# A four-block image model on one core: channels sorted by depth in the convolution attention, bands in two stages, and a linear attention in plain fp32

## The chip, the cores and the metric

One core of a Trainium2 chip. The metric is device time in microseconds (us) of one launch, median of several runs. A profile of one execution lists every instruction with its start and length. Engines: PE is TensorE (PEld its weight loads, which run beside its matmuls), DVE is VectorE, ACT is ScalarE, POOL is GpSimd, SP is SyncE, which only issues DMAs here. SBUF is the on-chip memory with 128 rows, PSUM the accumulator memory with eight banks of 512 fp32 values per row.

## The reference

x has the shape (32, 64, 16, 16): 32 pictures, 64 channels, 256 positions. All is fp32.

```
x = x + pe                                    # pe = pos @ W.T + b, the same for all pictures
x = x + conv_attention(group_norm(x))
t = tokens(x)                                 # (32, 256, 64)
t = t + causal_attend(layer_norm(t))          # softmax scan over the 32 pictures
t = t + mixture(layer_norm(t))                # 16 experts, top 2, hidden 128
t = t + linear_attention(layer_norm(t))
t = t + mixture(layer_norm(t))
```

The two that the change touches most:

```
# conv_attention: 8 heads of depth 8, C = 64
q, k, v = xt @ Wq.T + bq, xt @ Wkv.T + bkv (two halves)
q, k = (relu(q) + 1e-6) / scale, (relu(k) + 1e-6) / scale
q, k = q**3 / |q**3| * |q|, k**3 / |k**3| * |k|
out = per head: (q @ (k.T @ v)) / (q @ sum(k) + 1e-6)
out = out + conv5x5(v, per depth: the same kernel for all heads) + dwc_b
y = out @ Wproj.T + bproj

# linear_attention: 8 heads of 64, N = 256 tokens of a picture
h = x @ qkv_w + qkv_b, seen as q, v of (B, H, 64, N)
attn = sum over n of q[d, n] * lunchbox[d, r] * scale      # (B, H, R, D)
res = einsum('bhrd,bhdn->bhnd', attn, v)                   # a gain per (b, h, d), times v
out = res.reshape(B, N, H * 64) @ proj_w + proj_b
```

## The kernel before, in words

The program is a chain of stages, each a block in which every engine has its own hand-written program; a barrier ends each block. Semaphores order the engines inside a block, and each engine works its list strictly in order. The activations X lie in SBUF with tokens on rows: X[p, q, par, (b c)], where q is a pair of pictures, par the parity of the position, b the picture in the pair and c the channel.

**stage_norm** (L54 to L224) loads x, adds the position term and computes the group norm. DVE sums statistics (L173, L176), the softplus of the scale (L163 to L192), the group means, then the scaled weights into `wqkv` and `wproj` (L203 to L208), the biases into `brow` (L211 to L215), the transposed taps into `rowk` (L217), and the scale of the norm (L219, L220). Then ACT (L142) and DVE (L224) write half each of the normalised `xn`. PE turns the weights (L151, L152), expands the taps (L154) and averages the statistics over pairs of channels (L157).

**stage_qkv** (L227 to L408). PE multiplies `xn` with the weights in plain fp32 (L272) and adds the biases as an fp32r product of two parts (L273), 32 times. DVE takes q and k out (L390), ACT takes v out into V (L334). Squares and sixth powers on ACT (L305, L311), the cube on POOL or, for the last group, on DVE (L364), norms on DVE (L400, L402), roots on ACT (L316, L317), and the factor on DVE and POOL (L371), in four groups. The 5x5 convolution is a matmul of V with band matrices T: PE makes the bands in eight sets of four matmuls (L284) from `rowk` and the selection `sely`, ACT copies them into T (L322), all after the last of the 32 products. After that PE does 16 convolutions (L295), each for one depth d and one output parity: two accumulating fp32 matmuls of 256 columns. The channel of V is (head, depth), so the columns of one depth lie 8 values apart. Two PSUM banks alternate, and convolution k waits until ACT has taken out convolution k - 2 (L328):

```
pe.matmul(ps[:, 4 + k % 2, 0:B * NH], T[:, pj, 2 * d + pi, :],
          V[:, :, pj, d:2 * C:HD], start=(pj == 0), stop=(pj == 1))
```

**stage_attend** (L411 to L564). SP loads a mask and the projection bias, then the expert weights of the first mixture and the zeros of the block buffers. PE makes k.T @ v per pair of pictures (L453), DVE masks it to blocks of heads, BD (L540, L541), PE turns q (L462), multiplies (L478), DVE divides (L553 to L557), POOL adds the convolution FM (L532), PE turns the result (L490) and projects it (L500, L501), DVE adds the bias and writes X (L546).

**stage_pool** (L684 to L831). Layer norm, tanh scores, and a scan over pictures on DVE (L828). The scan needs (channel, picture) order, BH. DVE adds BH to X for one parity and POOL for the other (L728), each in BH's order, so that X is read and written with a stride. SP also loads the weights of the linear attention here (load_linear, L1363 to L1375).

**stage_mixture** for the first mixture: routing for two halves of the tokens, indirect DMAs on POOL (L980) that scatter them to blocks, the blocks of experts on all engines, and gathers on POOL (L992).

**stage_linear** (L1378 to L1642) has two halves (parts) of 16 pictures, each in four chunks of four pictures. Between the halves stands the routing of the first half for the second mixture, after it POOL scatters beside the second half. In a half, DVE sums the tokens (L1586), PE makes the sums product (L1461), DVE the gains (L1588, L1590). Then, per chunk k and head h:

- PE: one plain fp32 matmul of 128 rows by 512 columns for head h (L1472); the weights `wv` are block-diagonal, so that both parities of the positions come out on one half of the rows each.
- DVE: bias and gain while taking it out (L1597); ACT: a copy rounded to fp32r, `vh` (L1537); DVE: the rest, `vl` (L1606).
- PE: the projection of the chunk before, 8 steps of two fp32r matmuls (L1485), for `vh` and `vl`, each of 512 columns taken with a stride of 4:

```
ins = pe.matmul(ps[:, 3 + 2 * (k % 2) + half, :], pw[:, jj].rearrange("p a c -> p (a c)"),
                v[:, half * 2048 + jj:(half + 1) * 2048:4],
                start=(jj == 0 and part == 0), stop=(jj == 3 and part == 1))
```

- ACT takes it out with the bias (L1545), PE transposes it (L1498), DVE adds it to X (L1615) in four instructions per chunk. `pw` holds the rounded weights and their rest side by side, and the two are summed by DVE when it adds the two column halves.

PE's list interleaves value (k+1, step), projection (k, step) and transpose (k-1, step).

The second **stage_mixture** routes the second half, scatters it and does all blocks. **stage_out** gathers the last results on POOL (L992), adds them, turns X and writes it out.

## Time and profile before

| what | us |
|---|---|
| median of 3 runs | 1475.98 (1475.4 to 1478.64) |
| span of the profiled execution, first to last instruction | 1099.1 |
| PE busy | 602.3 |
| DVE busy | 698.3 |
| ACT busy | 410.9 |
| POOL busy | 589.1 |

For the profiled execution only the span is listed, not a time of its own. The times that follow count from the start of the span. A row of the timeline gives the start, the length over the instructions that were merged in it, the engine, the line, the operation, what is written and read, the shape and the count, and in brackets how long the engine was idle before it and what ended that. The compiler turns one fp32 matmul into two instructions and an fp32r matmul or a transpose into one.

### The profile page before, as it was taken

Reading aid. Unit: us, or ns where it says so; the run is one execution under the profiler, and the core shown is the slowest. Engines: PE = TensorE matmul, PEld = TensorE weight load, DVE = VectorE, ACT = ScalarE, POOL = GpSimd, SP = SyncE. Lnnn points to the kernel's source line nnn. Section 1 sums busy time; section 2 is a strip of 40 time slices with the busy share of each in tenths; the row PEclk is TensorE's granted clock in tenths of the full one; section 3 lists DMA queues with packets and bytes.
Section 4 is the critical chain, followed back from the end, with each engine's and each line's share of the span. In section 5 each row is a group of like instructions: output and inputs, shape, how many; then the busy total and the mean of one; then the engine's idle time right before and its main releaser. Section 6 shows DMA issues by size and latency. Waiting matters only on the chain. (4 is left out here: it accounts for less than half of the span.)

```text
span 1099.1 us, 12315 instructions
## 1 busy us (share of the span) xinstructions
PE 602.3 (55%) x3397; PEld 478.4 (44%) x3397; DVE 698.3 (64%) x1125; ACT 410.9 (37%) x688; POOL 589.1 (54%) x558
## 2 busy tenths in 40 slices
PE   2789776213310588477279841598155884783000
PEld 2774773213310587477144431244044774772000
DVE  6482474686670598478877589775458893885111
ACT  1454225131300576467224232143135773771000
POOL 0242141420777778777477600677205777775775
PEclk9979887555555799699679865698557996996555
DMA  3000991000211698688261100011104985882211
GB/s 106 7 1 1 207 354 25 0 1 0 94 46 52 198 292 243 198 249 241 57 103 24 24 1 0 38 46 53 53 22 147 299 259 185 261 250 62 55 35 38
DMA packets 126199, 118.91 MB, mean 108 GB/s; under 512 B 24917, under 2 KB 111525, under 8 KB 126147
## 3 DMA queue, kind: packets, MB, share of 16 engines
q1 hardware_dynamic: 56104, 54.93, 16.5%
q10 hardware_dynamic: 53659, 38.16, 11.9%
q0 software_dynamic: 16384, 25.20, 8.4%
q8 instruction: 23, 0.38, 0.1%
q14 instruction: 29, 0.24, 0.1%
HBM read 42.73 MB, written 44.04 MB: 79 GB/s over the span
## 5 line engine op out<-in xcount | busy, mean ns | idle before, releaser
L980 POOL DMA_INDIRECT blocks_x<-L_ffnmhl,L_ffnslot x192 | 198.5, 1034 | 162.9 <-DVE L_ffnslot L1233 105.0
L992 POOL DMA_INDIRECT gy_last<-blocks_y,L_ffnslot x128 | 129.7, 1013 | 57.0 <-issue 38.4
L992 POOL DMA_INDIRECT L_ffngy<-blocks_y,L_ffnslot x128 | 128.1, 1001 | 39.0 <-issue 39.0
L1033 PE MATMUL L_ffnps<-ident,L_ffnxb 128*128 128x128 f32 x384 | 65.5, 300 | 128.3 <-DMA L_ffnxb<-blocks_x 118.6
L1249 DVE TENSOR_TENSOR L_ffnwr<-L_ffnwb,L_ffnwr 128x640 fp32r<-128x640 f32 x96 | 79.2, 826 | 69.7 <-ACT L_ffnwr L1102 68.9
L1049 PE MATMUL L_ffnps<-L_ffnxt,L_ffnwr 128*128 128x256 f32 x768 | 118.3, 299 | 3.0 <-ACT L_ffngate L1118 2.4
L980 POOL DMA_INDIRECT blocks_x<-L_ffnlhl,L_ffnslot x64 | 66.3, 1036 | 82.3 <-DVE L_ffnslot L1233 63.1
L1102 ACT CAST L_ffnwr<-L_ffnwb 128x640 fp32r<-128x640 f32 x96 | 69.8, 727 | 108.5 <-issue 86.5
L1033 PEld LDWEIGHTS L_ffnps<-ident,L_ffnxb 128*128 128x128 f32 x384 | 44.7, 151 | 138.7 <-issue 107.8
L1049 PEld LDWEIGHTS L_ffnps<-L_ffnxt,L_ffnwr 128*128 128x128 f32 x768 | 101.4, 197 | 4.5 <-issue 3.2
L1060 PE MATMUL L_ffnps<-L_ffnwr,L_ffnhlo 128*128 128x128 f32 x384 | 92.8, 280 | 0.0
L1060 PE MATMUL L_ffnps<-L_ffnwr,L_ffnhh 128*128 128x128 f32 x384 | 88.6, 268 | 6.6 <-DVE L_ffnhlo L1262 6.2
L1256 DVE TENSOR_TENSOR L_ffnhid<-L_ffngate,L_ffnps 128x512 f32<-128x512 f32 x96 | 65.5, 686 | 34.4 <-ACT L_ffngate L1118 31.6
L1060 PEld LDWEIGHTS L_ffnps<-L_ffnwr,L_ffnhh 128*128 128x128 f32 x384 | 74.7, 195 | 8.7 <-issue 6.9
L1537 ACT CAST l_vh<-l_vg 128x512 fp32r<-128x512 f32 x64 | 39.6, 619 | 98.2 <-DVE l_vg L1597 98.2
L1060 PEld LDWEIGHTS L_ffnps<-L_ffnwr,L_ffnhlo 128*128 128x128 f32 x384 | 75.0, 195 | 0.0
L1113 ACT CAST L_ffnxt<-L_ffnps 128x512 fp32r<-128x512 f32 x96 | 56.2, 585 | 48.3 <-PE L_ffnps L1033 40.8
L1472 PE MATMUL l_ps<-l_xT,l_wv 128*128 128x512 f32 x128 | 71.7, 652 | 1.2
L1006 PE MATMUL L_ffnps<-ident,L_ffnmhl 128*128 128x128 f32 x96 | 22.5, 428 | 90.0 <-DVE L_ffnmhl L1175 66.6
L1272 DVE TENSOR_REDUCE L_ffnyb<-L_ffnps 128x256 f32<-128x512 f32 x96 | 65.8, 685 | 3.7 <-PE L_ffnps L1060 3.5
L1597 DVE SCALAR_TENSOR_TENSOR l_vg<-l_ps,lw_bv,l_gain 128x512 f32<-128x512 f32 x64 | 48.0, 751 | 29.7 <-PE l_ps L1472 29.7
L1262 DVE TENSOR_TENSOR L_ffnhlo<-L_ffnhid,L_ffnhh 128x512 fp32r<-128x512 f32 x96 | 66.2, 689 | 0.4
(289 smaller groups left out, 1387.4 us busy)
## 6 DMA issues: line engine op xcount, KB each, us to landing
L_ffnwb<-WR SPq DMA_DIRECT2D x192, 160.0 KB, 3.4
L_ffnxb<-blocks_x ACTq DMA_DIRECT2D x96, 256.0 KB
blocks_x<-zeros SPq DMA_DIRECT2D x2, 6144.0 KB, 29.9
blocks_y<-L_ffnyb ACTq DMA_DIRECT2D x96, 128.0 KB
WR<-in_L_ffn_w SPq DMA_DIRECT2D x10, 512.0 KB, 11.0
blocks_x<-L_ffnmhl,L_ffnslot POOLq DMA_INDIRECT x192, 2.2
Xc<-in_x SPq DMA_DIRECT2D x4, 512.0 KB, 7.5
L_ffngy<-blocks_y,L_ffnslot POOLq DMA_INDIRECT x128
```

Source lines behind the costliest of these rows:

```text
L980: pool.indirect_dma_start(self.XD[part], bass.IndirectOffsetOnAxis(self.slot[:, part, k, t:t + 1], 0), self.HL[part][:, t].rearrange("p a ...
L992: pool.indirect_dma_start(self.GY[part][:, k, t], None, self.YD[part], bass.IndirectOffsetOnAxis(self.slot[:, part, k, t:t + 1], 0)).then_ ...
L1033: ins = pe.transpose(ps[:, j % 2, s * P:(s + 1) * P], self.xb[:, j % 4, s], K["ident"][:])
L1049: ins = pe.matmul(ps[:, bank + j % 2, slots], self.wr[:, j % 4, k, b, c0:c0 + HID], x[:, slots], start=(k == 0), stop=(k == 1))
L1060: ins = pe.matmul(o, h[:, j % 2, s * P:(s + 1) * P], self.wr[:, j % 4, :, s * P // BS, 2 * HID:WC], start=(k == 0), stop=(k == 1))
L1102: act.copy(self.wr[:, j % 4, 0], self.wb[:, j % 4]).then_inc(self.w_hi, 1)
L1113: act.copy(self.xt[:, j % 2], ps[:, j % 2, :]).then_inc(self.xt_out, 1)
L1249: dve.tensor_tensor(self.wr[:, j % 4, 1], self.wb[:, j % 4], self.wr[:, j % 4, 0].bitcast(F32), ALU.subtract).then_inc(self.w_lo, 1)
L1256: dve.tensor_tensor(self.hid[:, j % 2], self.gate[:, j % 2], ps[:, 4 + j % 2, :], ALU.mult).then_inc(self.prod, 1)
L1262: dve.tensor_tensor(self.hlo[:, j % 2], self.hid[:, j % 2], self.hh[:, j % 2].bitcast(F32), ALU.subtract).then_inc(self.h_lo, 1)
L1272: dve.tensor_reduce(self.yb[:, j % 4].rearrange("p (s c) -> p s c", c=C), y, AX.X, ALU.add).then_inc(self.y_out, 1)
L1472: pe.matmul(ps[:, n % 2, :], wv[:, h].rearrange("p a c -> p (a c)"), xT[:, BC * (k % KP):BC * (k % KP + 1)].rearrange("p b n -> p (b n)"), ...
```

## The change

- Channels of q, k, v and of the weights, biases, masks and `wproj` are sorted as (depth, head) inside a picture instead of (head, depth). A new POOL copy sorts Wproj ahead of its transpose, and PE waits for it.
- Four of the eight band sets are made at the end of stage_norm, the other four between the products of stage_qkv (before products 16, 20, 24 and 28). `rowk` is written earlier; T and `sely` live over both stages.
- The convolutions use four PSUM banks instead of two. ACT takes the first eight out earlier in its list.
- The mask and the projection bias are loaded in stage_qkv instead of stage_attend.
- The add on X in stage_pool goes in the order of X; BH is read with a stride.
- Linear attention: weights loaded so that rows 0 to 63 and 64 to 127 hold the same thing. A value step is two plain fp32 matmuls of 64 rows, parity 0 on rows 0 to 63 and parity 1 on rows 64 to 127, into two banks, for two heads at once (32 pairs). No rounded copy and no rest. The projection is plain fp32, 8 matmuls per chunk instead of 16 in fp32r, the columns still with a stride of 4. The transpose becomes a plain fp32 matmul with a matrix `twin` (two identities stacked) that also adds the two row halves. DVE adds in two instructions per chunk. Two banks for the turned result instead of one set.

The diff, cut to its core:

```diff
@@ stage_norm
+                pool.wait_ge(big_w, 16 * 12)
+                pool.tensor_copy(w2[C:P].rearrange("p a (d h) -> p a d h", d=HD),
+                                 w3[C:P].rearrange("p a (h d) -> p a d h", d=HD)).then_inc(turned, 1)
...
+                for k in range(BANDS):
+                    bands(k)
                 act.wait_ge(norm_ready, 1)
...
+                pe.wait_ge(turned, 1)
                 pe.transpose(ps[:, 1, 0:P], w1[:].rearrange("p a c -> p (a c)"), K["ident"][:])
...
+                pe.wait_ge(sely_in, 16)
+                pe.wait_ge(rowk_sb, 1)
+                for k in range(BANDS):
+                    pj, i4 = k // 4, (k % 4) * 4
+                    for u in range(4):
+                        s0 = (HH - 1 - (i4 + u)) * 8
+                        ins = pe.matmul(ps[:, 4 + k, u * P:(u + 1) * P], sely[:, pj, s0:s0 + P],
+                                        rowk[:].rearrange("k d a b -> k (d a b)"), start=True, stop=True)
+                    ins.then_inc(band_ps, 1)
@@ stage_qkv
                 for i in range(NT2):
+                    if i >= 16 and i % 4 == 0:
+                        bands(BANDS + i // 4 - 4)
...
-                    if k >= 2:
-                        pe.wait_ge(conv_ev, k - 1)
+                    if k >= 4:
+                        pe.wait_ge(conv_ev, k - 3)
                     for pj in range(2):
-                        ins = pe.matmul(ps[:, 4 + k % 2, 0:B * NH], T[:, pj, 2 * d + pi, :],
-                                        V[:, :, pj, d:2 * C:HD], start=(pj == 0), stop=(pj == 1))
+                        ins = pe.matmul(ps[:, 4 + k % 4, 0:B * NH], T[:, pj, 2 * d + pi, :],
+                                        of_depth(V, pj, d), start=(pj == 0), stop=(pj == 1))
...
+                    if g >= 2:
+                        bands(BANDS + 2 * g - 4)
+                        bands(BANDS + 2 * g - 3)
                     act.wait_ge(qk_ev, (g + 1) * QG)
                     square(g)
                     if g == G - 1:
-                        bands(2)
+                        act.wait_ge(loaded, 16)
+                        conv(0)
+                        conv(1)
                     if g >= 1:
                         sixths(g - 1)
                     if g == G - 1:
-                        bands(3)
+                        for k in range(2, 5):
+                            conv(k)
@@ stage_attend
-                sp.dma_start(mask[:], A["k_mask"]).then_inc(loaded, 16)
...
-                dve.wait_ge(loaded, 48)
@@ stage_pool
-                eng.tensor_tensor(by_batch(X, par), by_batch(X, par),
-                                  BH[:, par].rearrange("p (c q b) -> p c q b", q=Q, b=2), ALU.add)
+                rows = X[:, :, par, :].rearrange("p q (b c) -> p q b c", b=2)
+                eng.tensor_tensor(rows, rows, BH[:, par].rearrange("p (c q b) -> p q b c", q=Q, b=2), ALU.add)
@@ stage_linear, PE
-                    pe.matmul(ps[:, n % 2, :], wv[:, h].rearrange("p a c -> p (a c)"),
-                              xT[:, BC * (k % KP):BC * (k % KP + 1)].rearrange("p b n -> p (b n)"), start=True, stop=True
-                              ).then_inc(v_mm, 1)
+                    for par in range(2):
+                        rows = slice(par * C, (par + 1) * C)
+                        pe.matmul(ps[:, n % 2 * 2 + par, :], wraw[rows, 1, h].rearrange("p a c -> p (a c)"),
+                                  xT[rows, BC * (k % KP):BC * (k % KP + 1)].rearrange("p b n -> p (b n)"),
+                                  start=True, stop=True).then_inc(v_mm, 1)
...
-                    for part, v in enumerate((vh, vl)):
-                        v = v[:, k % 2].rearrange("p h n -> p (h n)")
-                        ins = pe.matmul(ps[:, 3 + 2 * (k % 2) + half, :], pw[:, jj].rearrange("p a c -> p (a c)"),
-                                        v[:, half * 2048 + jj:(half + 1) * 2048:4],
-                                        start=(jj == 0 and part == 0), stop=(jj == 3 and part == 1))
+                    ins = pe.matmul(ps[:, 4 + k % 2, :], pwb[:, step].rearrange("p a c -> p (a c)"),
+                                    vg[:, k % 2, par].rearrange("p h n -> p (h n)")[:, jj:HP * BC * P:4],
+                                    start=(step == 0), stop=(step == H3 - 1))
...
-                    ins = pe.transpose(ps[:, (7, 2)[b // 2], step % 4 * P:(step % 4 + 1) * P],
-                                       oT[:, k % 2, b, par].rearrange("p h m -> p (h m)"), K["ident"][:])
+                    ins = pe.matmul(ps[:, 6 + k % 2, step * C:(step + 1) * C],
+                                    oT[:, k % 2, b, par].rearrange("p a h m -> p (a h m)"), twin[:], start=True, stop=True)
@@ stage_linear, DVE
-                def low(n):
-                    dve.wait_ge(vh_done, n + 1)
-                    dve.tensor_tensor(vl[:, n // H3 % 2, n % H3], vg[:, n % 4], vh[:, n // H3 % 2, n % H3].bitcast(F32),
-                                      ALU.subtract).then_inc(vl_done, 1)
+                    for par in range(2):
+                        dve.wait_ge(v_mm, 2 * n + par + 1)
+                        dve.scalar_tensor_tensor(
+                            out=vg[:, k % 2, par, h].rearrange("p (b n) -> p b n", b=BC),
+                            in0=ps[:, n % 2 * 2 + par, :].rearrange("p (b n) -> p b n", b=BC), scalar=bv[:, h:h + 1],
+                            in1=gain[:, h, BC * k:BC * (k + 1)].unsqueeze(2).to_broadcast([P, BC, P]),
+                            op0=ALU.add, op1=ALU.mult).then_inc(v_ev, 1)
```

## Rows read from the trace of the kernel before

**Rows 1.** The page: the span, and the chain that ended last by line.
```profile
span 1099.1 us, 12315 instructions
...
POOL gy_last L992 6%; DMA gy_last<-blocks_y,L_ffnslot 0%; DVE X L1310 0%; DVE gy_last L1309 0%; POOLq L1653 0%; PE o_ps L1665 0%; ACT o_y L1670 0%; DVEq L1303 0%; POOLq L1707 0%
```

**Rows 2.** Busy time by stretch: length, PE, PEld, DVE, ACT, POOL, PEclk, DMA, GB/s.
```profile
80.00:110.60 30.60, 29.77 (x64) 13.98 (x64) 8.89 (x9) 13.54 (x21) 5.90 (x2) 0.93 0.00 1
563.00:640.00 77.00, 66.90 (x162) 30.46 (x161) 51.40 (x87) 25.92 (x48) 51.06 (x50) 0.88 0.11 22
705.00:778.00 73.00, 63.69 (x157) 28.32 (x156) 47.75 (x79) 25.82 (x48) 56.10 (x55) 0.92 0.13 50
```

**Rows 3.** Convolution: two neighbouring weight loads in the timeline; its matmul by tile (min/median/max ns).
```profile
98.09 0.21 PEld L295 LDWEIGHTS q_ps<-V,q_t 128*128 128x128 f32 x1 [0.25 <-issue]
98.55 0.21 PEld L295 LDWEIGHTS q_ps<-V,q_t 128*128 128x128 f32 x1 [0.25 <-issue]
...
L295 PE MATMUL q_ps<-V,q_t x64: 638/640/787, 79.9 to 109.1; 128*128 128x256 f32 x64
```

**Rows 4.** Timeline, linear attention: weight loads four matmul instructions apart.
```profile
577.67 0.21 PEld L1472 LDWEIGHTS l_ps<-l_xT,l_wv 128*128 128x128 f32 x1 [0.25 <-issue]
...
579.45 0.21 PEld L1472 LDWEIGHTS l_ps<-l_xT,l_wv 128*128 128x128 f32 x1 [0.25 <-issue]
```

**Rows 5.** Timeline, first mixture: eight fp32r matmuls with contiguous columns.
```profile
462.23 1.20 PE L1049 MATMUL L_ffnps<-L_ffnxt,L_ffnwr 128*128 128x256 f32 x8
```

**Rows 6.** Timeline: start and end of both halves of the linear attention.
```profile
563.14 3.76 PE L1472 MATMUL l_ps<-l_xT,l_wv 128*128 128x512 f32 x4
...
636.07 1.54 DVE L1615 TENSOR_TENSOR X<-X,l_ps 128x256 f32<-128x256 f32 x4 [2.12 <-PE l_ps L1498]
...
698.55 3.56 PE L1461 MATMUL l_ps<-l_sx,l_wq 128*128 128x16 f32 x16 [13.81 <-DVE l_sx L1586]
701.96 1.20 PE L1472 MATMUL l_ps<-l_xT,l_wv 128*128 128x512 f32 x1
...
775.00 1.54 DVE L1615 TENSOR_TENSOR X<-X,l_ps 128x256 f32<-128x256 f32 x4 [1.81 <-PE l_ps L1498]
```

**Rows 7.** Timeline of stage_qkv: bands, the last evacuation, last scaling, last convolution.
```profile
64.09 3.89 PE L284 MATMUL q_ps<-rowk,q_sely 80*128 80x128 f32 x32
66.38 2.48 DVE L390 SCALAR_TENSOR_TENSOR q_qk<-q_ps,epsv 128x512 f32<-128x512 f32 x4
71.17 1.91 ACT L311 ACTIVATE q_s<-QKf 128x2048 f32<-128x2048 f32 x1
73.61 5.49 PE L284 MATMUL q_ps<-rowk,q_sely 80*128 80x128 f32 x24 [0.21 <-ACT q_t L322]
89.24 2.95 POOL L371 TENSOR_TENSOR QKf<-QKf,q_n 128x1024 f32<-128x1024 f32 x1 [0.28 <-DVE q_n L407]
109.81 0.72 ACT L328 ACTIVATE FM<-q_ps,q_dwb 128x256 f32<-128x256 f32 x1 [1.12 <-PE q_ps L295]
```

**Rows 8.** Linear attention by tile: DVE's and ACT's evictions, min/median/max ns.
```profile
L1597 DVE SCALAR_TENSOR_TENSOR l_vg<-l_ps,lw_bv,l_gain x64: 745/751/757, 565.3 to 760.0; 128x512 f32<-128x512 f32 x64
L1545 ACT ACTIVATE l_oT<-l_ps,lw_pbias x32: 465/467/475, 582.3 to 771.9; 128x256 f32<-128x256 f32 x32
```

**Rows 9.** Timeline, end of stage_norm: ACT's half of the normalisation.
```profile
29.11 4.04 ACT L142 ACTIVATE xn<-Xc,n_nmr,n_rs 128x256 f32<-128x256 f32 x8 [3.98 <-DVE n_nmr L220]
```

**Rows 10.** Timeline, stage_attend: DVE's first block product and PE behind it.
```profile
117.85 0.29 DVE L540 TENSOR_TENSOR a_bd<-a_ps,a_mask 128x128 f32<-128x128 f32 x1 [27.43 <-DMA a_bp<-in_L_conv_bproj]
...
118.28 2.09 PE L453 MATMUL a_ps<-V,QKf 128*128 128x129 f32 x8 [5.16 <-DVE a_bd L541]
```

**Rows 11.** Timeline, end of stage_pool: weighing and adding on DVE and POOL.
```profile
202.98 3.75 DVE L723 TENSOR_TENSOR p_bh<-p_h,p_co 128x2048 f32<-128x2048 f32 x1
...
203.14 8.91 POOL L723 TENSOR_TENSOR p_bh<-p_h,p_co 128x2048 f32<-128x2048 f32 x1 [33.47 <-DVE p_co L822]
...
216.41 9.89 POOL L728 TENSOR_TENSOR X<-X,p_bh 128x2048 f32<-128x2048 f32 x1 [4.36 <-DVE p_bh L828]
220.68 9.45 DVE L728 TENSOR_TENSOR X<-X,p_bh 128x2048 f32<-128x2048 f32 x1
```

300 lines of the change are left out of this document (149 added, 151 removed).

## The prediction

> **What bounds the kernel now.** I read the page first, then the busy time by stage, then the timeline inside the stages that the change touches, since shares over the whole span mix stages with different limits. The span is 1099.1 us [rows 1], the median of the runs is 1475.98 (1475.4 to 1478.64), so 376.9 us lie around the span. No time of its own is listed for the profiled execution; I take it to be the median one, leave what lies around the span as it is, and sum differences. The chain of work that ended last reaches back only to the last gather and says nothing of the stages in question [rows 1]. The work is a chain of stages with a barrier after each, so a stage is worth what its last engine gives up. In the convolution stretch PE is busy 29.77 of 30.6 us and in the two halves of the linear attention 66.90 of 77 and 63.69 of 73 [rows 2]: PE bounds all three. That is the fact on which this forecast hangs, because the change takes work from PE in the first and, by my count, adds it in the other two.
>
> **The prices.** A LDWEIGHTS starts when PE gets to the matmul before it, so the distance between weight loads is what one matmul instruction costs. In the convolution one of 256 fp32 columns with a stride of 32 bytes costs 0.46 us [rows 3]; the compiler makes two of every fp32 matmul (16 convolutions of two matmuls are the x64 of PE's row [rows 3]). In the linear attention four instructions come every 1.78 us, about 0.445 each: the two of one contiguous fp32 value matmul, 512 columns, and two fp32r projections of 512 columns with a stride of 16 bytes [rows 4]. An fp32r matmul of 256 contiguous columns costs (1.20 - 0.30) / 7 = 0.13 us [rows 5], so 512 contiguous columns would cost about 0.25. Two things follow. A contiguous fp32 instruction goes over its columns twice as long as an fp32r one, and a stride of 16 bytes or more doubles either: 0.46 per 256 strided fp32 columns, 0.92 per 512. That last figure is the price of the new projection and no row shows it directly; its ends are 0.44 (stride free in plain fp32) and 0.92 (as the convolution). I take 0.92, since the convolution is the same number format with the same kind of stride.
>
> **Linear attention, per half.** Now: from the first value matmul to the last residual 701.96 to 776.54, 74.6 us, and 563.14 to 637.61, 74.5 [rows 6]. After, per chunk of four batches: projections go from 16 fp32r to 8 plain fp32 matmuls, 16 instructions at 0.92 = 14.8 us (now 7.1); the values stay 8 matmuls, 16 instructions at 0.43 = 6.9 us (of the four distances in the 1.78 us I take the shorter for the contiguous ones; the granted clock of the halves is 0.88 and 0.92 of 2.4 GHz [rows 2]), if the row halves run one after the other; the 8 transposes become 8 fp32 matmuls with a summing matrix of 64 columns, 16 instructions bound by their weight loads, at (3.89 - 0.28) / 31 = 0.116 as the bands [rows 7], 1.8 us (now 0.9). The passes: values of chunk 0 alone, 6.9 + 1.6 for the start (an estimate: DVE is still busy with the gains) = 8.5; then chunk 1's values with projection 0, 21.6; twice with turns, 23.5 each; projection 3 with turn 2 and 0.3 of waiting, 16.9; the tail, four evictions of 0.47 [rows 8], 1.8 of turns, two residuals and latencies, 5.0. Sum 99.0, so +24.4. The cast and the subtraction per head (ACT and DVE) fall away; they are worth nothing, since DVE's remaining 32 evictions of 0.75 [rows 8] are 24 us under 93 of PE, and only in the first pass was DVE the limit (contained above). The sums matrix product halves from 16 instructions in 3.56 us [rows 6] and stands alone on the path: -1.7. Prepare on DVE: two memsets instead of one, fewer copies, +0.3 once. Serial halves: 2 x 22.7 + 0.3 = +46.
> The unknown is whether the row halves overlap. In order of issue they are a0, b0 (rows 0 to 63), a1, b1 (rows 64 to 127): only b0 and a1 can run side by side, because b0 must wait for a0 on the same rows; a pair then costs three instructions, 1.28 for 1.71, 16 pairs give 6.8 per half: +32. No row shows two row groups at work. I take the middle of the two, +39. The loads of the weights, 18 DMAs on SP for 10, are issued in the pool stage, long before it ends. The gather and the scatter that POOL works on beside these halves are done before the other engines ask for them, and longer halves only give them more time.
>
> **Norm and convolution stages.** Four of eight bands move into the norm stage. There ACT has to copy four bands (about 0.6 each) before its share of the normalisation, which starts at 29.11 [rows 9]; PE can only begin when DVE has copied rowk, moved up to about 25. At 0.116 per instruction the 32 instructions are done by 29, at the slow 0.22 of the later bands [rows 7] by 32: +0.6 to +3.5, taken as +2.0. The new POOL copy of Wproj stands ahead of PE's transposes and of POOL's own constants; it delays the group means on PE by less than DVE, busy with the softplus chain, comes late to them, so nothing; without that cover it would cost its own time, under 1 us. The other four bands stand between the QKV matmuls, PE without slack there: 32 x 0.116 = +3.7, and one wait of +1.2, since band 6 needs the bank that ACT frees only after copying V and band 4. PE is done with the products at 64.09 + 2.0 + 3.7 + 1.2 = 71.0 and DVE has the last of them out at about 71.9 instead of 68.9 [rows 7], and ACT's sixth powers of group 2 come after two evictions of the convolution, at 75.2 for 71.17: DVE's and POOL's chain through cube, norms and scale, which ends at 89.24 + 2.95 = 92.2 now, ends at about 96.3. The convolution can start at 72.2. Its moving operand is now runs of eight contiguous values. Ends: 0.46 per instruction as now, and 0.21 (half the contiguous 0.43). At 0.21, 64 instructions are 14 us, ACT's 16 evictions of 0.72 and the squares become the limit, and all is done by 94: the chain at 96.3 is late next. The break is at 0.36 per instruction. The stage ends at 96.3 instead of 110.6 (109.81 + 0.72 and the barrier [rows 7]): -14.3; at 0.46 PE would end at 101.7 and ACT at 102.5: -8.1. I take the first: in runs of eight, seven steps of eight go to the neighbouring value as in the contiguous operand, and only prices in the upper two fifths of that interval cost anything. The Trainium skill, "SBUF — State Buffer" (Door 1: The DMA port swizzle), says that SBUF is read in lines of 16 bytes and that only an access to a new line each time pays: by it too the runs are free and the stage gives 14.3.
>
> **Attention.** DVE stood until 117.85 for mask and bias, and PE's third product until 118.28 [rows 10], about 6 us after it could have started. Both are loaded a stage earlier, where SP has nothing to do: -6.2 (between -5 and -7). The first thing late after that is PE itself. Block matrix, z and y have the same element counts in another order: nothing.
>
> **Pool stage.** Add on X: DVE 9.45 us, ends the stage at 230.1; POOL 9.89, ends at 226.3 [rows 11]. With writes contiguous and one strided read they resemble the weighing, 3.75 on DVE and 8.91 on POOL: DVE ends at 224.4, POOL at 225.3: -4.8 (POOL unchanged: -3.8).
>
> **Sum.** -14.3 - 6.2 - 4.8 + 39 = +13.7: 1489.7, written 1490.
>
> **Rivals.**
> A, faster: the strided projection costs 0.44 per instruction in plain fp32, as its contiguous form. Then 64 x 0.48 = 31 us less per half, -62: 1427. For it: only the width of 256 columns has been seen. Against: both strided rows cost double. The change breaks even at 0.81 per instruction. 0.10.
> The same rule of the Trainium skill speaks against A, since a stride of 16 bytes meets a new line each time, whatever the format.
> B, faster: the row halves run wholly side by side, a pair for the price of one, 0.85. Against serial -13.7 per half: 46 - 27.3 - 25.3 = -6.6: 1469. It decides from a pair of 1.06 us down. Against: two instructions of one half share their rows. 0.07.
> The Trainium skill, "TensorE: Matmul & The Clock Gate" (Part 3: Packing small matmuls), is for it: matmuls on different row groups start nearly together. No row here shows it.
> C, slower still: the convolution keeps 0.46: +6.2, 1496. 0.15.
> D, slower still: every change between half rows and full rows costs PE the tail that otherwise overlaps, 0.64 - 0.46 = 0.18, what a convolution instruction lasts beyond its distance to the next [rows 3]; 32 changes per half on serial halves: 46 + 11.5 - 25.3 = +32, 1508. 0.08.
> "TensorEngine Tiling (Array Packing)" (Key Properties) of the Trainium skill says that a change of tiling mode drains the engine; it speaks against this change, and no run here has shown it.
>
> **Numbers.** The forecast has 0.60, with a range of its own of 1482 to 1498. The range that holds 8 in 10 leaves out A and reaches from B to D: 1468 to 1508. Within 0.2% (3 us, about what can be told from no change) lies little, only the seam between B and the forecast: 0.05. Faster: A and B, 0.17. Slower: 0.78.
>
> **What would show it.** In the profile after: LDWEIGHTS of the projection 0.92 apart (A: 0.44); first value matmul to last residual 92 to 99 us per half (A: about 65), PE over 90% busy, DVE under 45%; a value pair at 1.28 or 1.71 (B: 0.85); convolution loads 0.21 to 0.25 apart and POOL's last scaling ending the stage near 96; DVE's first block product within 1 us of the stage's start; the add on X under 5 us on DVE. The forecast is wrong if the halves get shorter, or if the gains before 230 us are under 15.

## The result, and the profile after

| | before, us | after, us | ratio (95% interval) |
|---|---|---|---|
| first comparison | 1477.31 (1475.4 to 1480.24, 4 runs) | 1460.98 (1454.15 to 1466.1, 4 runs) | 0.9885 (0.9848 to 0.9922) |

The forecast said 1490 and slower. The change is faster by 16 us, 1.15%, and outside the range of 1468 to 1508.

The first thing to read in the profile after is the span, and then, in the page's second part, the strips of 40 slices (each digit a tenth of busy time):

```profile
span 1464.3 us, 12163 instructions
PE 664.5 (45%) x3445; PEld 500.0 (34%) x3445; DVE 652.8 (45%) x1044; ACT 368.4 (25%) x624; POOL 569.7 (39%) x558
DVE  6567396404304920399203297111550294019611
ACT  2442322200204710383000140000320273018300
POOL 0424050771772067202760004740057404740375
```

The span is 1464.3 us, and this execution's own time is 1466.1. So what lies around a span is 1.8 us, not the 376.9 us that the forecast put there. The profile of before [rows 1], span 1099.1, shows an execution of another kind than those that were timed. The strips show what it lacks: wherever POOL stands at 7 (it issues its indirect DMAs), DVE goes to 0 to 4 and ACT to 0 to 2.

Where no indirect DMA runs, the steps can be read as forecast. Convolution: its matmul and ACT's eviction by tile (min/median/max ns), for [rows 3] and the last row of [rows 7]:

```profile
L348 PE MATMUL q_ps<-V,bands x64: 378/379/796, 74.6 to 94.0; 128*128 128x256 f32 x64
L381 ACT ACTIVATE FM<-q_ps,q_dwb x16: 454/473/487, 76.1 to 94.4; 128x256 f32<-128x256 f32 x16
```

The matmul lasts 0.379 us for 0.640, the eviction 0.473 for 0.72. Timeline of the other steps of the first 211 us, for [rows 9, 10, 11]:

```profile
24.98 7.17 PE L193 MATMUL n_ps<-rowk,sely 80*128 80x128 f32 x32 [2.88 <-DVE rowk L238]
...
32.67 4.04 ACT L169 ACTIVATE xn<-Xc,n_nmr,n_rs 128x256 f32<-128x256 f32 x8
...
98.85 0.29 DVE L588 TENSOR_TENSOR a_bd<-a_ps,mask 128x128 f32<-128x128 f32 x1 [2.82 <-PE a_ps L501]
...
197.58 9.54 POOL L778 TENSOR_TENSOR X<-X,p_bh 128x2048 f32<-128x2048 f32 x1 [4.36 <-DVE p_bh L876]
201.85 8.76 DVE L778 TENSOR_TENSOR X<-X,p_bh 128x2048 f32<-128x2048 f32 x1
```

The bands take 7.17 us for 32 instructions, 0.22 each, the slow end; ACT's normalisation starts at 32.67 for 29.11. DVE's first block product is at 98.85 for 117.85. The add on X is only a little shorter, 8.76 for 9.45 on DVE and 9.54 for 9.89 on POOL. The stages up to here give 19.5 us (DVE's first work of the mixture at 210.9 for 230.4); POOL's last scaling ends the convolution stage at 97.80, for the forecast 96.3.

Linear attention, for [rows 4]: weight loads of one steady iteration, two heads' values and two projections.

```profile
911.96 0.30 PEld L1522 LDWEIGHTS l_ps<-l_xT,lw_wraw 64*128 64x128 f32 x4 [1.70 <-issue]
...
913.02 0.30 PEld L1533 LDWEIGHTS l_ps<-l_vg,l_pwb 128*128 128x128 f32 x2 [0.76 <-issue]
...
913.99 0.21 PEld L1533 LDWEIGHTS l_ps<-l_vg,l_pwb 128*128 128x128 f32 x1 [0.67 <-issue]
914.89 0.21 PEld L1533 LDWEIGHTS l_ps<-l_vg,l_pwb 128*128 128x128 f32 x1 [0.69 <-issue]
...
916.79 0.30 PEld L1522 LDWEIGHTS l_ps<-l_xT,lw_wraw 64*128 64x128 f32 x4 [1.70 <-issue]
```

The projection that comes next has its weights loaded 913.02 - 911.96 = 1.06 us after the first of the four value instructions (64 rows, 512 columns, two per parity), and the projections go at 0.90 (914.89 - 913.99), as forecast. But 1.06 is not all that the pair costs: the load of the next value comes 1.90 us after the last load of a projection. The whole iteration takes 916.79 - 911.96 = 4.83 us at a granted clock of 1.00, and less four projections of 0.90 that leaves 1.23 for the pair. But the busy time by stretch, for [rows 2] (length, PE, PEld, DVE, ACT, POOL, PEclk, DMA, GB/s), is nothing like before's 67 us of 77:

```profile
701.00:764.00 63.00, 29.67 (x49) 7.96 (x49) 9.40 (x14) 0.00 (x0) 47.21 (x50) 0.63 0.15 28
764.00:837.50 73.50, 62.71 (x144) 22.66 (x144) 17.25 (x29) 6.63 (x16) 0.00 (x0) 0.88 0.00 1
900.00:975.00 75.00, 42.96 (x86) 11.84 (x85) 13.93 (x21) 1.66 (x4) 56.58 (x59) 0.77 0.13 52
975.00:1026.30 51.30, 46.07 (x108) 16.55 (x108) 11.94 (x21) 4.97 (x12) 0.00 (x0) 0.90 0.00 0
```

Each pair is one half, up to the end of POOL's list and behind it. In the first half's 63 us beside the list PE issues 49 matmuls, in the 73.5 behind it 144.

### The profile page after: what moved, and what is told of

It is laid out like the page before. It is cut to its first block and busy times, and to the rows that moved or that the text cites. A ratio compares the mean times of both kernels' runs of the same rounds, so it can differ in the third digit from the quotient of the medians.

```text
span 1464.3 us, 12163 instructions
## 1 busy us (share of the span) xinstructions
PE 664.5 (45%) x3445; PEld 500.0 (34%) x3445; DVE 652.8 (45%) x1044; ACT 368.4 (25%) x624; POOL 569.7 (39%) x558
## 5 line engine op out<-in xcount | busy, mean ns | idle before, releaser
L1028 POOL DMA_INDIRECT blocks_x<-L_ffnmhl,L_ffnslot x192 | 191.4, 997 | 232.5 <-DVE L_ffnslot L1281 174.9
L1097 PE MATMUL L_ffnps<-L_ffnxt,L_ffnwr 128*128 128x256 f32 x768 | 132.1, 322 | 151.9 <-issue 108.3
L1097 PEld LDWEIGHTS L_ffnps<-L_ffnxt,L_ffnwr 128*128 128x128 f32 x768 | 114.0, 220 | 157.1 <-issue 111.5
L1108 PE MATMUL L_ffnps<-L_ffnwr,L_ffnhh 128*128 128x128 f32 x384 | 98.0, 287 | 135.3 <-DVE L_ffnhlo L1310 105.3
L1533 PE MATMUL l_ps<-l_vg,l_pwb 128*128 128x512 f32 x128 | 128.1, 1101 | 7.4 <-issue 7.3
L1108 PE MATMUL L_ffnps<-L_ffnwr,L_ffnhlo 128*128 128x128 f32 x384 | 101.2, 297 | 0.0
L1108 PEld LDWEIGHTS L_ffnps<-L_ffnwr,L_ffnhlo 128*128 128x128 f32 x384 | 82.0, 214 | 0.0
L1590 ACT ACTIVATE l_oT<-l_ps,lw_pbias 64x256 f32<-64x256 f32 x32 | 13.3, 462 | 265.6 <-PE l_ps L1533 137.1
L1166 ACT ACTIVATE L_ffngate<-L_ffnps 128x512 f32<-128x512 f32 x96 | 57.5, 601 | 71.5 <-remote 54.3
L1522 PE MATMUL l_ps<-l_xT,lw_wraw 64*128 64x512 f32 x128 | 45.6, 807 | 64.1 <-DVE l_vg L1636 40.4
L1054 PE MATMUL L_ffnps<-ident,L_ffnmhl 128*128 128x128 f32 x96 | 23.0, 428 | 113.7 <-issue 58.8
```

The lines of the kernel that those rows point to most:

```text
L1028: pool.indirect_dma_start(self.XD[part], bass.IndirectOffsetOnAxis(self.slot[:, part, k, t:t + 1], 0), self.HL[part][:, t].rearrange("p a ...
L1097: ins = pe.matmul(ps[:, bank + j % 2, slots], self.wr[:, j % 4, k, b, c0:c0 + HID], x[:, slots], start=(k == 0), stop=(k == 1))
L1108: ins = pe.matmul(o, h[:, j % 2, s * P:(s + 1) * P], self.wr[:, j % 4, :, s * P // BS, 2 * HID:WC], start=(k == 0), stop=(k == 1))
L1166: act.activation(self.gate[:, j % 2], ps[:, 2 + j % 2, :], ACT.Silu).then_inc(self.silu, 1)
L1533: ins = pe.matmul(ps[:, 4 + k % 2, :], pwb[:, step].rearrange("p a c -> p (a c)"), vg[:, k % 2, par].rearrange("p h n -> p (h n)")[:, jj:H ...
```

## The experiments

**The kernel before once more, the two parts of the change apart, and the changed kernel without indirect DMAs.** The first run has no edit. The second and third take the diff up to and with the add on X (the mask's constant among it), and stage_linear with its loads, each on the kernel before. The fourth replaces, in scatter and gather, as below, and puts both into SP's list (`pool` in these functions is then SP):

```diff
-                pool.indirect_dma_start(self.XD[part], bass.IndirectOffsetOnAxis(self.slot[:, part, k, t:t + 1], 0),
-                                        self.HL[part][:, t].rearrange("p a c -> p (a c)"), None
+                rows = slice((k * TH + t) * P, (k * TH + t + 1) * P)
+                pool.dma_start(self.XD[part][rows, :], self.HL[part][:, t].rearrange("p a c -> p (a c)")
```

> The kernel before, unchanged, profiled again. What is in doubt is the 376.9 us that the forecast put around the span. Theory S: they are inside the span. The profile of before shows an execution of 1099.1 us in which no engine stands still without cause, while the timed ones last 1477; in the profile after (1464.3 us) ACT, DVE and PE stand still for 10 to 80 us at a time while POOL issues its indirect DMAs. Then a second profile of before may show a span of 1470 to 1478 with the time about 2 us above it, and with idle time put down to 'remote' or 'issue' beside POOL's lines 978 to 990. Rival O: the 377 us lie outside the span for this kernel; then the span is again about 1099 with a time of about 1476 beside it, and the stalls are something that only the change brings.

> The changes of the norm, convolution, attention and pool stages alone (channels by depth, bands in two stages, four banks, mask preloaded); the linear attention is that of before. Against the two profiles the first 211 us gave 19.5 us. Theory S: those stages hold no indirect DMA, so their gain is the same in a timed execution: 1477.3 - 19.5 = 1458 us, within 4. Rival W: the waits beside POOL's indirect DMAs are of varying length and swallow it: 1468 to 1480. Rival L: the linear attention carries the gain of 16 us and the front nothing: 1475.

> The linear attention of the change alone (plain fp32, parities on separate row halves), all other stages as before. The forecast was +39 us; the profile after shows the strided projections at the forecast 0.92 us an instruction, but a pair of row halves at 1.05 for 1.28. Theory S: the stage has 32 evictions of DVE per half and no cast and subtraction, so fewer handovers between engines, each of which can be late while POOL issues its gathers and scatters; additive with the front's -19.5 of a total of -16.3 gives +3: 1480 us, within 5. Rival P: PE's extra work stands undiminished: 1477.3 + 25 to 39 = 1502 to 1516, and then the front would have to give over 40. Rival L: the linear attention itself is faster, 1460.

> The changed kernel with each indirect DMA of POOL (512 of 128 rows) replaced by a plain DMA of the same 128 rows on SP's queue. Left out is the placing of the rows by their slots: tokens go to consecutive rows and come back from them; all arithmetic of the engines stays. Theory S: POOL's indirect DMAs make the others stand still, so without them the stalls go, and the time is near the undisturbed execution: 1099 - 19 + 10 to 40 for the linear attention, less what waits for POOL's lists themselves (about 80 us each before units start): 900 to 1120 us. Rival O: the stalls come from something else (a state of the core, code loading): over 1350 us.

Measured, beside the kernel before at 1476.1 us (1460.5 to 1483.6): 1481.5 for the first (one execution), with a span of 1479.9; front 1455.9, ratio 0.9878 (0.9829 to 0.9928); linear 1481.0, ratio 1.0051 (1.0021 to 1.0082); without indirect DMAs 1085.4 (one execution, with wrong results, since the rows are not placed). Theory S held in all four (the span is 2 us above its range): the 377 us are stalls inside the span, they come with POOL's indirect DMAs, the front gives all of the gain, the linear attention costs 5 us. The fourth run changes the kind of DMA and the engine that issues it together, so it doesn't tell which of the two matters. The page of the kernel before in this kind of execution, to be set beside the one that stands ahead of the prediction:

```profile
span 1479.9 us, 12315 instructions
PE 649.3 (44%) x3397; PEld 508.1 (34%) x3397; DVE 698.0 (47%) x1125; ACT 410.5 (28%) x688; POOL 571.0 (39%) x558
DVE  5645757701601940199515697125650293029611
ACT  2542323200201830183203231012320282027300
POOL 0422331574474047401770005730057305730375
```

The two halves of its linear attention by stretch, up to POOL's list's end and behind it; they belong beside the four rows of after:

```profile
717.00:780.00 63.00, 26.10 (x38) 9.06 (x38) 14.75 (x23) 6.80 (x11) 47.65 (x50) 0.61 0.14 26
780.00:843.00 63.00, 50.33 (x124) 23.74 (x124) 34.84 (x60) 19.22 (x37) 0.00 (x0) 0.83 0.00 1
907.00:981.00 74.00, 33.06 (x55) 12.45 (x54) 19.59 (x31) 10.11 (x17) 56.43 (x58) 0.68 0.13 51
981.00:1037.10 56.10, 40.94 (x108) 19.39 (x108) 29.47 (x51) 15.98 (x31) 0.00 (x0) 0.83 0.00 1
```

And what a stall looks like in the timeline (first half, POOL issues a DMA every 1.26 us all the while):

```profile
749.10 0.75 DVE L1597 SCALAR_TENSOR_TENSOR l_vg<-l_ps,lw_bv,l_gain 128x512 f32<-128x512 f32 x1 [4.25 <-remote]
...
749.89 0.62 ACT L1537 CAST l_vh<-l_vg 128x512 fp32r<-128x512 f32 x1 [4.98 <-issue]
749.91 1.13 PE L1472 MATMUL l_ps<-l_xT,l_wv 128*128 128x512 f32 x2 [2.62 <-issue]
750.47 1.02 PE L1485 MATMUL l_ps<-l_vh,l_pw 128*128 128x512 f32 x1
...
751.29 0.66 PE L1485 MATMUL l_ps<-l_vl,l_pw 128*128 128x512 f32 x1
...
759.59 0.75 DVE L1597 SCALAR_TENSOR_TENSOR l_vg<-l_ps,lw_bv,l_gain 128x512 f32<-128x512 f32 x1 [9.12 <-remote]
...
770.79 0.75 DVE L1597 SCALAR_TENSOR_TENSOR l_vg<-l_ps,lw_bv,l_gain 128x512 f32<-128x512 f32 x1 [9.85 <-issue]
...
781.99 0.75 DVE L1597 SCALAR_TENSOR_TENSOR l_vg<-l_ps,lw_bv,l_gain 128x512 f32<-128x512 f32 x1 [9.85 <-remote]
```

DVE evicts a value at 749.10, ACT's cast of it starts at 749.89 and PE's next value matmul at 749.91: two handovers in under 0.1 us after DVE's end. PE is through at about 752. DVE, for which a finished value lies ready, starts at 759.59, and then every 11.20 us. Over all lists of this trace I took the waits of over 0.15 us beside POOL's DMAs that only one engine could end, and counted from that engine's last instruction to the waiting one. From PE to DVE or ACT there are 59, 28 of them over 1 us late, the longest 38.5; between DVE and ACT 23, none over 0.04 us; from DVE or ACT to PE 36, none over 0.15. In the first profile [rows 1] the 129 from PE took at most 0.11. (The counts hang on which waits are taken; the longest and the difference between the engines do not.) So it is what comes from PE that is late. The ends of matmuls are modelled in the profile, so it doesn't tell whether PE's results or only the signals of them come late. They do so after a while: on time for the first 10 to 34 us of a list, then mostly by 0.5 to 5 us, then by 5 to 38. In the last stage, where PE does four transposes every 20 us, they come on time though POOL's list runs:

```profile
1434.67 1.09 PE L1665 MATMUL o_ps<-ident,X 128*128 128x128 f32 x4 [19.27 <-DVE X L1310]
1435.79 0.61 ACT L1670 COPY o_y<-o_ps 128x512 f32<-128x512 f32 x1 [19.75 <-issue]
```

**Pauses in POOL's list, plain DMAs in the kernel before, and more matmuls without more handovers.** Edits:

```diff
@@ scatter (gather alike, after every 8 DMAs)
                                         ).then_inc(self.scattered[part], 16)
+                if (t + 1) % 8 == 0:
+                    pool.wait_ge(self.scattered[part], 16 * (k * TH + t + 1))
@@ stage_linear, value(n), the run with more matmuls
+                    if n % (KP * H3) < 20:
+                        for _ in range(2):
+                            pe.matmul(ps[:, n % 2, 0:P], wv[:, h].rearrange("p a c -> p (a c)"),
+                                      xT[:, BC * (k % KP)], start=True, stop=True)
                     pe.matmul(ps[:, n % 2, :], wv[:, h].rearrange("p a c -> p (a c)"),
```

> The kernel before with each of POOL's 512 indirect DMAs replaced by a plain DMA of 128 rows on SP's queue, as was done to the changed kernel (that one took 1085.4 us, its halves of the linear attention 89.7 and 90.0 us from first value matmul to last residual). Left out is the placing of the rows by their slots. Theory S (the forecast held for an execution without stalls): the halves are those of the first profile, 74.5 us each, the first stages 19.5 us longer; 1085.4 - 31 - 2 of lost sums + 19.5 = 1072 us, so here the change as a whole is 11 to 14 us slower. Rival F: the change is faster without the stalls as well: over 1090 us.

> The changed kernel; POOL waits after every 8 indirect DMAs until these have landed (8 waits a list of 64, about 2 us each). In the stalled profiles handovers from DVE and ACT beside POOL's lists arrive in 0.03 to 0.15 us, and only those from PE come late, on time at first and then by 3 to 19 us in steps of 0.7 us, as if the completions of PE stood in a queue that is served slowly while POOL issues one indirect DMA every 1.27 us. Theory Q (a queue that fills and drains in a pause): every pause empties it, most of the 375 us of stalls go, against 8 x 8 x 2 = 130 us of longer lists of which about half are covered: 1120 to 1300 us. Theory H (each handover of PE beside an indirect DMA is late for itself): the pauses help only what falls into them, and the lists get longer: 1480 to 1560 us.

> The same pauses in the kernel before. Theory Q: 1110 to 1290 us, and since the other engines then work beside the lists, the linear attention's extra work of PE shows: the change (against the run above) is no longer 16 us faster but the same or up to 14 us slower. Theory H: 1490 to 1570 us and the change stays about 16 us faster.

> The kernel before with two more matmuls of 128 columns ahead of each of the first 20 value matmuls of a half of the linear attention, into the bank that the value matmul then overwrites: 4 more instructions of PE for 4 to 6 now between two handovers, and not one more handover. Read is the distance between DVE's evictions of values in the second half of POOL's list, now 5.6 and then 11.2 us. Theory Q (what waits in the queue are PE's instructions, not its handovers): about twice as long, 11 to 22 us, and fewer evictions beside the list. Theory H: the distances stay 5.6 and 11.2 us, and each half takes 3 to 5 us longer for the instructions' own time.

Measured, the kernel before at 1482.8 us: with pauses 1287.0, 1297.3, 1308.6 and 1313.0 (after; no ratio is on record for so wide a spread) and 1307.0 (before; ratio to no pauses 0.8825, 0.8794 to 0.8856). Theory Q held in that the pauses take most of the stalls away, against H. Its numbers did not: 1307 lies above its 1110 to 1290, and the change was to be the same or up to 14 us slower, and its median is 4 us below 1307. The traces show what hides the longer second half (89.7 us for 74.0): in both kernels POOL's list with its pauses now ends the stage, and the next stage's first instruction comes 21.9 us after the last residual before and 5.4 us after it in the changed kernel. By the count above, of 109 handovers from PE beside a list 15 were over 1 us late in the changed kernel, the longest 4.6 us, and 20 of 124 in the one before, the longest 5.1; for 28 of 59 and 38.5 without pauses. (The expectation of the run with a wait after every 4 says that none was late any more; that was a miscount of mine.) With pauses (a value every 1.89 us beside the list, POOL's wait among it):

```profile
701.85 0.75 DVE L1601 SCALAR_TENSOR_TENSOR l_vg<-l_ps,lw_bv,l_gain 128x512 f32<-128x512 f32 x1 [0.54 <-PE l_ps L1476]
...
702.64 1.38 POOL L994 DMA_INDIRECT gy_last<-blocks_y,L_ffnslot  x1 [1.78 <-DMA gy_last<-blocks_y,L_ffnslot]
...
703.74 0.75 DVE L1601 SCALAR_TENSOR_TENSOR l_vg<-l_ps,lw_bv,l_gain 128x512 f32<-128x512 f32 x1 [0.54 <-PE l_ps L1476]
...
705.64 0.75 DVE L1601 SCALAR_TENSOR_TENSOR l_vg<-l_ps,lw_bv,l_gain 128x512 f32<-128x512 f32 x1 [0.54 <-PE l_ps L1476]
```

The halves of the linear attention took 74.6 and 74.0 us before and 89.9 and 89.7 after, from the first value matmul to the last residual. With plain DMAs it was 74.3 and 74.6 against 89.7 and 90.0, and the whole 1079.4 against 1085.4 (one execution each). My 1072 for the former was 7 off. The linear attention isn't the reason: the next stage starts at 773.30 for 788.16, 14.9 us apart. Of these 8.9 are gone at the end of the span, in the stages behind; what takes them back I didn't find out.

The run with more matmuls took 1507.2 us, +24, and its distances grew:

```profile
759.51 0.75 DVE L1601 SCALAR_TENSOR_TENSOR l_vg<-l_ps,lw_bv,l_gain 128x512 f32<-128x512 f32 x1 [15.45 <-remote]
...
760.31 1.23 PE L1474 MATMUL l_ps<-l_xT,l_wv 128*128 128x128 f32 x4 [13.87 <-issue]
761.33 1.92 PE L1476 MATMUL l_ps<-l_xT,l_wv 128*128 128x512 f32 x2
...
776.31 0.75 DVE L1601 SCALAR_TENSOR_TENSOR l_vg<-l_ps,lw_bv,l_gain 128x512 f32<-128x512 f32 x1 [15.45 <-remote]
```

16.80 us with six matmul instructions in between, 11.20 with four: 2.8 us per instruction of PE in both, with the same one handover. The four instructions between late evictions of the changed kernel's first routing gave 11.20 too (L1054 x4, ACT's L1139 at 306.38, 317.58, 328.78, 339.98). Theory H, a price per handover, falls. What fits is a queue of PE's completions: 40 to 92 matmul instructions are issued in a list before it holds anyone up by over 5 us (beside the second half 48 in the kernel before; in the changed one the first late handover, by 3.2 us, came after 62), then it lets one through in 2.8 us, and POOL's pause of 1.8 us takes most of it away. Earlier in a list the distance was 5.6 us for the same four, so 2.8 is the rate of the full queue only. What the queue is, no run here shows. All timed executions have a recorded span and clock, so no run tells either whether the stalls would come without that recording. The Trainium skill, "NOTIFIC — the notification-queue block" (7.1 Overflow), describes records of the engines whose full ring can stall the engine that writes them; nothing here tells whether that is it. The Trainium skill, "SBUF — State Buffer" (A bandwidth-pool intuition that's wrong), says that GpSimd can't write its descriptors until DVE releases the port that they share; that rule doesn't fit, since POOL's DMAs kept their pace (64 in 82 us, 86 in the first profile), DVE's own instructions their 0.75 us, and ACT waited as well.

**How often to pause, and where.** On the kernel with the first stages of the change, no pause in the last list; the third is the changed kernel.

> The first stages of the change with the linear attention of before, POOL waiting for its DMAs after every 8 of them in all lists but the last (in the last stage the handovers of PE came in time without pauses). With pauses the kernel before took 1307 us. Theory Q: 1307 - 19.5 for the first stages - 11 for the seven pauses of about 1.6 us that leave the last list = 1277 us. Rival: the start of the lists shifts against the other work and stalls come back, or the last list needs its pauses too: over 1290.

> The same with a wait after every 16 indirect DMAs (20 us of POOL's list between two waits instead of 10). In the unbroken lists the first late handover came 15 to 27 us after the list's start. Theory Q: the queue is nearly full before the pause; where PE issues much the stalls come back in part, which weighs more than the 28 pauses saved (28 x 1.6 = 45 us in all lists, some 25 on the path): 1270 to 1350 us. Theory T (only time since the last pause matters, not what PE issued): all stalls stay away: 1255.

> The changed kernel with the same pauses, none in the last list. Against the first run of this batch it differs in the linear attention alone. Without stalls its halves are 15.3 us longer each (89.9 and 89.7 for 74.6 and 74.0), the sums 1.8 shorter each. Theory S: the first half's 13.5 us stand in the time; in the second POOL's list with its pauses (about 93 us) ends after the last residual in either form and covers part: 14 to 27 us slower than that run. Rival N: POOL's lists bound both halves, no difference: within 5 us.

> As the first run of this batch with a wait after every 4 indirect DMAs. Theory Q: at every 8 no handover of PE was over 1 us late any more, so more waits only lengthen the lists: 8 more waits of about 1.6 us in each of seven lists, 13 us a list, of which some five stand on the path: about 1340 us. If it is no slower than every 8, stalls were left there.

These fell on another chip, and there the kernel before took 1099.6 us (1095.7 to 1104.4). Of the five chips that the runs of this section were made on, three had stalls (that of the first four runs, that of the next four, and that of the first three under the next heading) and two had none (this one, which had none again in the changed kernel's second run there, and that of the last two runs); no chip showed both kinds. So the stalls go with the chip or with how it is set up, and not with the kernel, and the first profile looks like one from a chip without. None of my times fits, since all were made from 1307. Without stalls a pause is pure cost: every 16 1120.0 (ratio 1.019, 1.014 to 1.024), every 8 1163.5 (1.060, 1.055 to 1.065), every 4 1233.2 (1.121, 1.116 to 1.126). The changed kernel with every 8 took 1175.3, 11.8 more than the front alone with the same pauses, for the expected 14 to 27. (The three ratios are to the kernel before, so the front's gain is in them.)

**The change and its parts on both kinds of chip.** No edits.

> The changed kernel once more, beside the kernel before on the same chip. In the last batch the kernel before took 1099.6 us (1095.7 to 1104.4 in 7 runs) where it had taken 1476 to 1483 in the batches ahead of it: the stalls belong to the chip or its setting, not to the kernel. Theory S: on a chip where the kernel before takes about 1100, the first stages give 19.5, the linear attention costs about 2 x 15.3 less 2 x 1.8 for the sums, less what POOL's lists cover: the change is 0 to 10 us slower, ratio 1.000 to 1.010. On one where it takes about 1477 it is faster by 16 us again, ratio 0.989. Rival: ratio about 0.985 to 0.99 on either.

> The first stages of the change alone. No list of indirect DMAs stands in them, so the gain is the same 19 us on either kind of chip: 1080 where the kernel before takes 1100 (ratio 0.982), 1457 where it takes 1477 (0.987).

> The linear attention of the change alone. Where the kernel before takes 1100: the halves 74.5 to 90, +27 less what POOL's scatter list covers in the second half (in the first profile that list ended 1 us after the last residual, so nothing much): 1119 to 1127, ratio 1.018 to 1.025. Where it takes 1477: +4 to +9 as before. Rival: the same +5 on either kind of chip.

> The changed kernel beside the kernel before on whatever chip this is. Where the kernel before takes about 1100 us: ratio 1.000 to 1.010 by the stages' own durations (first stages -19.5, linear attention +27 at most). Where it takes about 1477: 0.989 to 0.992 as in the two comparisons so far.

> The first stages of the change with the linear attention of before. The whole change gave 1097.6 for 1099.2 us on a chip without stalls: its second half of the linear attention hid behind POOL's scatter list, the first did not (14.6 us). Where the kernel before takes about 1100 us: 17.5 us less, 1082, ratio 0.984 (0.981 to 0.987), so better than the whole change there too. Where it takes about 1480: 0.988 as in the two comparisons so far.

The last two fell on chips without stalls, each with its own runs of the kernel before.

| | with stalls (before 1476 to 1482) | without (before 1097 to 1099) |
|---|---|---|
| the change | 0.9924 (0.9894 to 0.9953) | 0.9991 (0.9962 to 1.0019) |
| first stages alone | 0.9888 (0.9858 to 0.9918) | 0.9828 (0.9773 to 0.9883) |
| linear attention alone | 1.0048 (1.0025 to 1.0070) | not measured |

The expected ratios were 0.989, 0.987, 1.003 to 1.006, 1.000 to 1.010 and 0.984; none is off by more than 0.4%. Without stalls the change does nothing to the time, 1097.6 for 1099.2 us. Without stalls the front alone beats both kernels, 1078.7 beside 1097.4 for the kernel before. With stalls it beats the kernel before, 1455.9 and 1467.0; against the whole change, 1469.4 on the same chip as the 1467.0, the difference isn't clear of noise.

> The same with POOL waiting for its DMAs after every 16, in all lists but the last. On the chip without stalls this took 1120.0 us for 1099.6 of the kernel before (ratio 1.019). There: the same again. Where the kernel before takes about 1480, waits after every 8 in all lists gave 1307 us: theory Q: 16 DMAs are 20 us of list, the stalls come back only where PE issues much: 1170 to 1290 us. Rival: 1350 and more, the queue is full after 10 us already.

It fell on a chip without stalls, the one of the run before it: 1124.6 (1.024, 1.019 to 1.029), for 1.019 the first time. How long a list may run on a chip with stalls between pauses was thus not measured.

The profile of the changed kernel without stalls has a span of 1098.7 for 1099.1 [rows 1]. Its halves, for [rows 6]:

```profile
545.67 2.93 PE L1522 MATMUL l_ps<-l_xT,lw_wraw 64*128 64x512 f32 x6
...
634.07 0.75 DVE L1647 TENSOR_TENSOR X<-X,l_ps 128x256 f32<-128x256 f32 x2 [3.00 <-PE l_ps L1546]
...
697.56 2.93 PE L1522 MATMUL l_ps<-l_xT,lw_wraw 64*128 64x512 f32 x6
...
786.42 0.75 DVE L1647 TENSOR_TENSOR X<-X,l_ps 128x256 f32<-128x256 f32 x2 [4.03 <-PE l_ps L1546]
788.08 1.22 DVE L676 TENSOR_REDUCE L_ffns<-X 128x16 f32<-128x1024 f32 x1 [0.90 <-PEq L1732]
```

First half 545.67 to 634.8, 89.1 us for 74.5; second 697.56 to 787.2, 89.6 for 74.6. The last row is the next stage's first instruction, 0.90 us after the last residual. In the trace of before the same place reads:

```profile
776.59 0.97 POOL L980 DMA_INDIRECT blocks_x<-L_ffnlhl,L_ffnslot  x1 [0.30 <-issue]
787.65 1.22 DVE L627 TENSOR_REDUCE L_ffns<-X 128x16 f32<-128x1024 f32 x1 [11.10 <-PEq L1707]
```

DVE stood 11.10 us, since POOL's scatter list ended the stage: its last DMA began at 776.59, a tenth of a microsecond after DVE was done, and took 0.97, and the next stage started 10.1 us behind it. The front alone without stalls shows 10.1 us again, and all seven profiles with pauses, whose lists end late too, 11.5. After, that list is over at 771.7 and its 10 us are covered by the longer half. So the next stage starts at 788.08 for 787.65: of 15.0 us, 10.2 were hidden, and the other 4.8 used up the 4.4 us by which the half began earlier.

## Why the prediction was wrong

**The step that failed** is the first: "No time of its own is listed for the profiled execution; I take it to be the median one, leave what lies around the span as it is, and sum differences." 376.9 us around a span were the sign that it was not the median one. Times around the spans are 1.8 us, and the timed executions hold some 380 us of stalls. What is between POOL's lists stands at its old price there, what is beside them does not. In the stalled executions from the end of POOL's list to the last residual it was 63.3 us before and 74.3 after in the first half (+11.0), 56.2 and 51.9 in the second (-4.3), +6.7 for the two, where the forecast had +39. Over all seven profiles with unbroken lists and stalls (three with the old linear attention, four with the new) the means of the two stretches differ by +12.5 and -1.3. With -19.5 the +6.7 makes -12.8 of the measured -16.3. The other 3.5 can't be given to a place: the routing ahead of the first list took 44.2 to 49.0 us in executions of one and the same code (44.3 in the profile of before with stalls, 49.0 in the one of after), the whole of the changed kernel 1454 to 1466.

That the second half lost nothing agrees with a queue that counts instructions: the changed kernel's projection does 0.90 us of work in each, the old one 0.44, so it got from 900.2 to 929.6 before it was held up, 29 us of the 89 that it takes without stalls, and the kernel before from 907.2 to 925.7, 18.5 of 74.5. This is how I read it; no run changes the size of an instruction alone.

**Where the forecast's own kind of execution was measured** (1099.2 before), it was too high by 15 us, and the step errors are these:
- Pair of row halves: 1.23 us (4.83 of an iteration less 4 x 0.90), for an estimate between 1.28 and 1.71. So a half should take 99.0 - 16 x 0.48 - 64 x 0.02 = 90.0, and took 89.1 and 89.6. That 1.23 lies near 1.28 is luck, since the reason given for it ("only b0 and a1 can run side by side") is wrong. In the pass that has values only, the halves run wholly side by side, as rival B (chance 0.07) had it: at a granted clock of 0.50 two instructions, one on each half, pass in 547.54 - 546.69 = 0.85 us, and in the kernel before one full-row instruction took 564.99 - 564.13 = 0.86 at that clock. First after, without stalls, then before:

```profile
546.69 0.34 PEld L1522 LDWEIGHTS l_ps<-l_xT,lw_wraw 64*128 64x128 f32 x2 [0.51 <-issue]
547.54 0.34 PEld L1522 LDWEIGHTS l_ps<-l_xT,lw_wraw 64*128 64x128 f32 x2 [0.51 <-issue]
...
564.13 0.34 PEld L1472 LDWEIGHTS l_ps<-l_xT,l_wv 128*128 128x128 f32 x1 [0.52 <-issue]
564.99 0.34 PEld L1472 LDWEIGHTS l_ps<-l_xT,l_wv 128*128 128x128 f32 x1 [0.52 <-issue]
```

  The four instructions of a pair are thus 1.70 us at half the clock, 0.85 at the full one (an estimate). Between projections the pair costs 0.38 more, 0.19 for each of its two changes between half rows and full rows, and rival D had 0.18 for such a change. B and D were each right about one thing, and neither time came. The Trainium skill, "TensorE: Matmul & The Clock Gate" (Part 3: Packing small matmuls), had said that matmuls on different row groups start nearly together, and this trace agrees with its 0.85. "TensorEngine Tiling (Array Packing)" (Key Properties) of the Trainium skill had said that a change of mode drains the engine, and the 0.19 agrees with that.
- "The gather and the scatter that POOL works on beside these halves are done before the other engines ask for them": false in the second half. Its list ended with the half, and 10.2 us of the extra were covered.
- The projection at 0.92: 0.90. Right, and rival A fell.
- Convolution -14.3: -12.7. PE's instructions went at 0.22 for the forecast 0.21, and rival C fell; ACT's eviction took 0.473, where I had kept 0.72. But the bands in the norm stage cost +3.6 (products begin at 37.0 for 33.4), where I took +2.0 out of +0.6 to +3.5.
- Attention -6.2: -6.2.
- Add on X -4.8: -0.7. One strided read cost nearly what the strided read and write had, and the row of the weighing was no measure for it.
- First stages in all -25.3: -19.5. Sums: 1.86 us for 3.56, as forecast.

With these: -17.5 at the first half's start, +14.6 for that half and -1.6 for the sums make -4.4 at the second half's start, and of its +15.0 only 4.8 are seen: +0.4 at the next stage's first instruction, and 1098.7 for 1099.1 in the spans.

## What to carry to other kernels

Set the profile's span beside its own time before anything is priced from it; when the timed median is a third longer than the span, the profile shows another kind of execution, and the first thing wanted is a second profile. Beside long lists of indirect DMAs a kernel may run in two ways, and a change beside them has to be timed on both: here the same edit gives 1% on one kind of chip and nothing on the other, and only the part away from the lists gives on both. A stage that a barrier ends is as long as its last engine, POOL's landing DMAs included, so look at the next stage's first instruction and not at the last one of the engine in question.

## What was not expected of the hardware

- On some chips PE's completions reach ACT and DVE late, by up to 38 us in the profile of the kernel before, beside POOL's unbroken indirect DMAs (one in 1.26 us), one PE instruction per 2.8 us; in the first profile, with the same kernel and the same DMAs, within 0.11. It makes 1477 us of 1099.
- There, a wait of POOL for its own DMAs after every 8 (1.8 us) takes 12% off the time, and on the other kind of chip it adds (every 8, all but the last list; the two times are of two such chips) 1163.5 - 1078.7 = 85 us to the front alone.
- Where POOL's list was the last thing of a stage, the next stage's first instruction came 10.1 us behind its last indirect DMA (two profiles), and 11.5 where the list had pauses (seven).
- Two matmuls of 64 rows on the two row halves pass in the time of one of 128 rows, but each change between such a pair and full-row matmuls costs 0.19 us, so a pair between projections takes 1.23 us and not 0.85.
